# Cross-attention queries by head with the weights stationary, four batches at a time, in place of batch by batch

## The reference

```python
x = _layernorm(x + _L0_attn_ref(x, w_q, w_k, w_v, w_o), axis=-1)
# cross-attention, 16 heads of 128
q = (hidden_states @ Wq + bq).reshape(b, s, NH, HD).transpose(0, 2, 1, 3)
q = _rmsnorm(q, qn_w)      # q * rsqrt(mean(q*q) + 1e-6) * qn_w, for each token and head
scores = jnp.einsum('bhsd,bhed->bhse', q, k) * scale
```

## Time and profile before

| | us |
|---|---|
| median of three runs | 1571.53 |
| the profiled execution | 1568.75 |
| its span, first to last instruction | 1566.9 |
| TensorE busy | 1454.7 (93%) |
| VectorE busy | 951.6 (61%) |
| ScalarE busy | 662.6 (42%) |
| GpSimd busy | 647.5 (41%) |

### The profile page before, as it was taken

One profiled execution on the slowest core, in us unless ns is written; L12 is line 12 of the kernel. 1 busy time (PEld: TensorE's weight loads), 2 busy tenths in 40 slices (PEclk: granted clock), 3 DMA queues, 4 the chain that ended last, 5 costly groups with the idle time before them and its releaser, 6 DMA issues. The chain is left out here.

```text
span 1566.9 us, 25497 instructions
## 1 busy us (share of the span) xinstructions
PE 1454.7 (93%) x8673; PEld 1178.6 (75%) x8673; DVE 951.6 (61%) x3585; ACT 662.6 (42%) x1789; POOL 647.5 (41%) x1000
## 2 busy tenths in 40 slices
PE   7999999999988889999999999999999999399976
PEld 7677767767766678888888888888888887277854
DVE  3766566566566676556655566556655574743357
ACT  4444343343352444344444444444434445243246
POOL 1334234334334454434444444434443435264164
PEclk9999999999999999999999999999999999699999
DMA  6311221221232431121111121211212113485363
GB/s 211 117 64 64 95 74 64 96 74 64 82 129 74 161 109 46 60 62 56 55 44 62 57 64 35 72 56 56 61 44 62 57 42 113 153 239 163 110 215 119
DMA packets 60790, 140.43 MB, mean 90 GB/s; under 512 B 10165, under 2 KB 20761, under 8 KB 59666
## 3 DMA queue, kind: packets, MB, share of 16 engines
q1 hardware_dynamic: 56086, 123.85, 23.8%
q0 software_dynamic: 4576, 14.95, 3.5%
HBM read 94.31 MB, written 44.46 MB: 89 GB/s over the span
## 5 line engine op out<-in xcount | busy, mean ns | idle before, releaser
L1281 POOL TENSOR_TENSOR b_pcarry<-b_half 128x1 f32<-128x1 f32 x173 | 47.1, 273 | 382.0 <-DVE b_rinv L1151 343.8
L1039 ACT ACTIVATE b_probs<-b_probs,b_nmax 100x361 f32<-100x361 f32 x256 | 152.0, 594 | 72.5 <-DVE b_nmax L1145 72.1
L71 PE MATMUL bank<-b_kTh,b_q 128*100 128x362 f32 x512 | 171.2, 335 | 6.4 <-issue 4.8
L1145 DVE CUSTOM_DVE_ANT_0 b_probs<-bank,b_mask 100x361 f32<-100x361 f32 x256 | 135.5, 529 | 49.9 <-issue 41.8
L1306 POOL TENSOR_SCALAR b_probs<-b_probs,b_rinv 100x361 f32<-100x361 f32 x256 | 163.5, 651 | 0.0
L1138 DVE TENSOR_TENSOR b_pTl<-bank,b_pTh 121x400 fp32r<-121x400 f32 x192 | 109.8, 572 | 52.4 <-ACT b_pTh L1034 52.4
L1034 ACT ACTIVATE b_pTh<-bank 121x400 fp32r<-121x400 f32 x192 | 96.7, 504 | 92.6 <-PE bank L871 87.9
L1080 ACT ACTIVATE b_oTh<-bank,b_bv 128x400 fp32r<-128x400 f32 x64 | 38.1, 595 | 222.6 <-PE bank L71 222.6
L871 PE MATMUL bank<-ident,b_probs 100*121 100x100 f32 x768 | 109.7, 265 | 4.3 <-POOL b_probs L1306 3.3
L871 PEld LDWEIGHTS bank<-ident,b_probs 100*121 100x121 f32 x768 | 106.9, 185 | 6.8 <-POOL b_probs L1306 4.5
L71 PE MATMUL bank<-b_Woh,b_oTh 128*100 128x512 f32 x256 | 110.6, 432 | 1.4 <-DVE b_oTl L1209 1.4
(11 more groups left out here) (259 smaller groups left out, 3901.0 us busy)
## 6 DMA issues: line engine op xcount, KB each, us to landing
b_q<-q_d SPq DMA_DIRECT2D x64, 400.0 KB, 3.2
q_d<-a_qo SPq DMA_DIRECT2D x62, 400.0 KB, 2.4
b_ctxr<-in_ctxT SPq DMA_DIRECT2D x48, 242.0 KB, 4.0
y_d<-c_y SPq DMA_DIRECT2D x32, 256.0 KB
c_Eraw<-in_expert_w SPq DMA_DIRECT2D x10, 512.0 KB, 7.4
a_stage<-in_Wq SPq DMA_DIRECT2D x4, 1024.0 KB
stage<-in_Wo SPq DMA_DIRECT2D x8, 512.0 KB, 4.5
a_xTr<-in_xT SPq DMA_DIRECT2D x8, 400.0 KB
```

Of the source, the lines that this page charges most:

```text
L71: mm = eng.matmul(out, lhsT=l(c), rhs=r(c), start=first and k == 0, stop=last and k == n - 1)
L1039: act.activation(p, p, ACT.Exp, scale=-1.0, bias=nmax[:, s % 2, h:h + 1], accum_out=psums[:, s % 2, h:h + 1]).then_inc(e_rdy, 1)
L1145: dve.tensor_tensor_reduce(out=probs[:, s % 2, h, 0:SE], in0=s_bank[h % 2][0:S, 0:SE], in1=mask_s[:], scale=-1.0, scalar=BIG, op0=ALU.add, ...
L1281: pool.tensor_tensor(pcarry[:, k:k + 1], half_s[:, 0:1], half_s[:, 0:1], ALU.add)
```

## The change

The query projection no longer goes with one batch. It waits until four batches (400 tokens, `GT`) have their normed rows, kept transposed and split in `x1Th`, `x1Tl` (two sets). Then it goes by heads: 64 steps m, 16 for each group of four batches. In `query_head(m)` the 128 columns of Wq of one head are the weights and the 400 tokens move; the result stands with the head's 128 values on the partitions, so no transposes are needed. VectorE adds the bias (`queries`), ScalarE and GpSimd each square it (`squares_hi`, `squares`), VectorE takes the difference as the low part (`squares_lo`), and two products with a matrix of ones (`square_sums`) put the sum of squares on every partition. ScalarE takes the root as logarithm and exponential (`root_log`, `root_exp`), VectorE scales (`scaled_queries`), ScalarE writes the high part (`queries_hi`) and GpSimd the low one (`queries_lo`). SP stores two heads at a time in four DMAs of 200 KB, in runs of 800 bytes.

Batches 0 to 3 have no heads, batch 4 has three, each later one four (`heads(i)`), and 17 are left behind the last batch, with the splits of the next phase's context and weights and its three key products among them. The loop of batches is written out. The next pair's projection stands whole behind PV. The bias comes as 128 x 16.

```diff
+GB, HB = 4, 4
+GT = GB * S
+KV_FRAME, CTX_FRAME = (50, 52, 56, 58), (48, 50, 55)
...
+        def heads(i):
+            return [m if m >= 0 else None for m in range(HB * (i - GB) - 1, HB * (i - GB) + HB - 1)]
+        def q_bank(m):
+            return bank[4 + m % 2]
+        def ss_bank(m):
+            return q_bank(m) if m < TAIL else bank[2 + m % 2]
...
+            def store_q(p):
+                sp.wait_ge(q_lo, 2 * p + 2)
+                group, kv, half = p // 8, p // 2 % 4, p % 2
+                for b in range(GB):
+                    dst = q_d[(GB * group + b) * XKV + kv][:, :, half * 2 * S:(half + 1) * 2 * S]
+                    sp.dma_start(dst, qo[:, p % 2, b].bitcast(F32)).then_inc(q_out[p % 2], 16)
...
+            sp.wait_ge(v_done, B)
+            for n in range(2):
+                sp.dma_start(head_raw[:, n], head.pieces[n][0]).then_inc(head.w_raw[n], 16)
+            sp.wait_ge(x1_rdy, B)
+            sp.dma_start(x1_d[B - 1], x1_s[:]).then_inc(x1_out, 16)
+            sp.wait_ge(oT_done, B)
+            sp.wait_ge(qx_done, XH * (B // GB - 1))
+            for n in range(2):
+                sp.dma_start(head.ctxr[:, n], ctxT[n]).then_inc(head.ctx_in[n], 16)
+            for m in range(TAIL, NQ):
+                if m % 2:
+                    store_q(m // 2)
+                for n in range(2):
+                    if m == KV_FRAME[n] + 3:
                         sp.wait_ge(head.w_lo, n + 1)
-                        sp.dma_start(head.pieces[2 + n][1], head.pieces[2 + n][0]).then_inc(head.w_raw[n], 16)
-                if is_int and i == B - 1:
+                        sp.dma_start(head_raw[:, n], head.pieces[2 + n][0]).then_inc(head.w_raw[n], 16)
+                if m == CTX_FRAME[0] + 3:
                     sp.wait_ge(head.ctx_lo, 1)
...
+            def query_head(m):
+                group, kv, cols = m // XH, m // XG % XKV, slice(m % XG * XHD, (m % XG + 1) * XHD)
+                if m % XH == 0:
+                    pe.wait_ge(x1T_lo, GB * (group + 1))
+                if group == 0 and m % XG == 0:
+                    pe.wait_ge(w_lo, 3 + kv)
+                if m >= TAIL + 2:
+                    pe.wait_ge(q_ev, m - 1)
+                elif m >= 2:
+                    pe.wait_ge(ln_set, m - 1)
+                product3(pe, q_bank(m)[:, 0:GT], lambda c: Wqh[:, kv, c, cols], lambda c: Wql[:, kv, c, cols],
+                         lambda c: x1Th[group % 2][:, c, :], lambda c: x1Tl[group % 2][:, c, :], range(DC)).then_inc(qx_done, 1)
+            def square_sums(m):
...
+                pe.wait_ge(sq_hi, m + 1)
+                if m >= TAIL + 2:
+                    pe.wait_ge(ln_set, m - 1)
+                pe.wait_ge(sq_lo, m + 1)
+                pe.matmul(ss_bank(m)[:, 0:GT], lhsT=ones_r[:], rhs=qsh[:], start=True, stop=False)
+                pe.matmul(ss_bank(m)[:, 0:GT], lhsT=ones_r[:], rhs=qsl[:], start=False, stop=True).then_inc(ss_done, 1)
...
+                if m[0] is not None:
+                    if m[0] >= 1:
+                        square_sums(m[0] - 1)
+                    query_head(m[0])
...
+                if m[1] is not None:
+                    query_head(m[1])
+                    if m[0] is not None:
+                        square_sums(m[0])
...
+                if m[2] is not None:
+                    query_head(m[2])
+                pe.wait_ge(v_ev, i + 1)
+                pe.wait_ge(pt_ev, 4 * i + SR)
...
+                if m[1] is not None:
+                    square_sums(m[1])
+                if pair + 1 < NPAIR:
+                    if par == 0:
+                        project(pair + 1, wk_s, range(DC), wk_in)
+                    else:
+                        project(pair + 1, wq_s, range(DC), wq_in)
+                if m[3] is not None:
+                    query_head(m[3])
+                    square_sums(m[2])
...
+            t = TAIL
+            square_sums(t - 1)
+            query_head(t)
+            keep_busy(pe, bank[3][:, 0:P], ident_s, 8)
+            transpose_x1(B - 1)
+            keep_busy(pe, bank[3][:, 0:P], ident_s, 8)
+            for m in range(t + 1, NQ):
+                query_head(m)
+                square_sums(m - 1)
+            context_keys(0)
+            square_sums(NQ - 1)
+            context_keys(1)
+            context_keys(2)
...
+            def squares_hi(m):
...
+                act.wait_ge(q_ev, m + 1)
+                wait(act, ss_done, m)
+                act.activation(qsh[:], qb[:, m % 2], ACT.Square).then_inc(sq_hi, 1)
+            def root_log(m):
...
+                act.wait_ge(ss_done, m + 1)
+                wait(act, q_rdy, m - 1)
+                act.activation(qrs[:, m % 2], ss_bank(m)[:, 0:GT], ACT.Ln, bias=rms_eps_s[:, 0:1]).then_inc(ln_set, 1)
+            def root_exp(m):
...
+                act.wait_ge(ln_set, m + 1)
+                act.activation(qrs[:, m % 2], qrs[:, m % 2], ACT.Exp, scale=-0.5).then_inc(qrs_set, 1)
+            def queries_hi(m):
...
+                act.wait_ge(q_rdy, m + 1)
+                p = m // 2
...
+                if m % 2 == 0:
+                    wait(act, q_out[p % 2], 16 * GB * (p // 2))
+                act.activation(qo[:, p % 2, :, 0, m % 2 * S:(m % 2 + 1) * S], qn[:, m % 2].rearrange("p (b t) -> p b t", b=GB),
+                               ACT.Copy).then_inc(q_hi, 1)
...
+                root_log(before)
+                root_exp(before)
+                exponent(i, 0)
+                exponent(i, 1)
+                if i >= 1:
+                    rows_hi(i - 1)
+                squares_hi(m[0])
+                queries_hi(before - 1)
+                exponent(i, 2)
+                exponent(i, 3)
+                if i == 1:
+                    split_hi(5)
+                act.wait_ge(v_done, i + 1)
+                act.activation(v_s[:], bank[7][0:S, :], ACT.Copy).then_inc(v_ev, 1)
+                root_log(m[0])
+                probs_T(i, 0)
+                probs_T(i, 1)
+                squares_hi(m[1])
+                root_exp(m[0])
+                probs_T(i, 2)
+                probs_T(i, 3)
+                if i == 0:
                     split_hi(2)
+                queries_hi(before)
+                squares_hi(m[2])
+                act.wait_ge(oT_done, i + 1)
+                act.activation(oTh[:].rearrange("p c t -> p (c t)"), bank[7][:, 0:DC * S], ACT.Copy).then_inc(oT_hi, 1)
+                root_log(m[1])
+                root_exp(m[1])
+                queries_hi(m[0])
+                if par == 1 and pair + 1 < NPAIR:
                     scaled_q(pair + 1, 0)
                     scaled_q(pair + 1, 1)
                     split_xT(pair + 1)
+                if i == 0:
                     split_hi(3)
                     split_hi(4)
+                queries_hi(m[1])
+                squares_hi(m[3])
+                root_log(m[2])
+                root_exp(m[2])
+            t = TAIL
+            root_log(t - 1)
+            root_exp(t - 1)
+            queries_hi(t - 2)
+            squares_hi(t)
+            queries_hi(t - 1)
+            rows_hi(B - 1)
+            for m in range(t + 1, NQ):
+                squares_hi(m)
+                root_log(m - 1)
+                root_exp(m - 1)
+                if m >= t + 2:
+                    queries_hi(m - 2)
+                if m in KV_FRAME:
+                    context_weights_hi(KV_FRAME.index(m))
+            root_log(NQ - 1)
+            root_exp(NQ - 1)
+            queries_hi(NQ - 2)
+            queries_hi(NQ - 1)
...
+            def queries(m):
...
+                dve.wait_ge(qx_done, m + 1)
+                wait(dve, q_rdy, m - 1)
+                dve.tensor_scalar(qb[:, m % 2], q_bank(m)[:, 0:GT], bq_s[:, m % XH:m % XH + 1], None, ALU.add).then_inc(q_ev, 1)
+            def squares_lo(m):
...
+                dve.wait_ge(sq_hi, m + 1)
+                dve.wait_ge(sq_set, m + 1)
+                dve.tensor_tensor(qsl[:], qsq[:], qsh[:].bitcast(F32), ALU.subtract).then_inc(sq_lo, 1)
+            def scaled_queries(m):
...
+                wait(dve, q_lo, m - 1)
+                dve.wait_ge(qrs_set, m + 1)
+                dve.scalar_tensor_tensor(out=qn[:, m % 2], in0=qb[:, m % 2], scalar=qkw_s[:, 3:4], in1=qrs[:, m % 2],
+                                         op0=ALU.mult, op1=ALU.mult).then_inc(q_rdy, 1)
...
+                    residual(i - 1)
+                masked(i, 0)
+                if i >= 1:
+                    statistics(i - 1)
+                masked(i, 1)
+                scaled_queries(before)
+                if i >= 1:
+                    apply_norm(i - 1)
+                masked(i, 2)
+                invert_sums(i, 0)
+                masked(i, 3)
+                queries(m[0])
+                invert_sums(i, 1)
+                if i >= 1:
+                    rows_lo(i - 1)
+                if i == 1:
+                    split_lo(4)
+                invert_sums(i, 2)
+                squares_lo(m[0])
+                invert_sums(i, 3)
```

(70 more changed lines are left out.)

540 lines of the change are left out of this document (202 added, 338 removed).

## The result

The changed kernel takes 1593.33 us (median of four runs, 1589.74 to 1599.89) against 1571.91 us for the kernel before on the same chip: a ratio of 1.0135, 95% interval 1.011 to 1.016, so slower. The forecast was 1592. The profiled execution took 1589.74 us (span 1587.9), 21.0 us more span than before.

A forecast was written before the change was run, and what follows sets the result against it. TensorE's own work was taken to bound a batch. 44.3 + 68.5 + 25.5 + 9 x 27.65 + 7 + 47.4 = 441.6 us, with the tail 540.6, 20.4 later than before: forecast 1592 us, range 1553 to 1612.

The forecast's parts named there:

- the tail: Behind the last batch's output product: 17 heads, splits, late loads and final stores take 99 us, against 31.2 before.
- Batches without heads: Batches 1 to 3: the softmax chain is bare, 22.2 us a batch including 2 for the clock; together 68.5.
- Batches with heads: Batches 5 to 13: four heads each, 27.65 us, TensorE's work 24.9 of it, plus 0.7 a batch for the clock.
- 43 us less work: First phase, TensorE: cheaper query products and no query transposes, less the added products with ones, net 43 us.
- The input load behind the stores: Batches with heads, SP queue: an input load sits behind the query stores, charged 1 us in all.
- The loop was put at 3.5 us: Tail: one head's eviction, square, log, exponential, scale and split in turn take 3.44 us, plus 0.06 for the port.
- VectorE's back-to-back pair isn't broken into: SBUF port: whichever engine begins first keeps the other out, so GpSimd can't get between two consecutive VectorE instructions.
- splits and loads with the clock behind them: Tail: context and weight splits and two late weight loads (+5.9 each) add 20.5 us, the clock 6 more.
- The 6 us for the clock: Tail: TensorE stands still for up to 5 us at splits and loads, so its clock falls, +6 us.
- A: Whole kernel, faster: few port collisions, clock holds, loads in time; batches 27.0, tail 76, time 1554 us; chance 0.25.
- B: Whole kernel, slower: every batch trips the clock fully and the head's chain runs late; batches 29.5, time 1609; chance 0.2.
- C: Whole kernel, in between: loads on time and half of the clock losses gone cancel the rest, 1572 us; chance 0.1.

The follow-up runs named there:

- e4: Changed kernel, with the next input load issued between the two halves of the odd batches' stores from batch 5 on; ratio 1.0019 to the kernel before.
- e2: Changed kernel, with GpSimd behind the last batch waiting for head m's low squares before the low part of query head m-2; ratio 1.0089 to the kernel before.
- e7: Changed kernel with e1, e3, e4, context loads first and GpSimd's context split behind its squares and low part; 1555.36 us, ratio 0.9897 to the kernel before.
- e5: Changed kernel with e1 and e3 together; ratio 0.9998 to the kernel before.
- e10: e7 with GpSimd's context split between its squares of head m and low part of head m-2; 1544.57 us, ratio 0.9866 to the kernel before.
- e12: The kernel of e10 run once more, on one chip with e11; 1543.58 us, ratio 0.9872 to the kernel before.
- e3: Changed kernel, with the third and fourth weight pieces loaded as soon as their buffer half is free; ratio 1.0070 to the kernel before.
- e1: Changed kernel, with VectorE behind the last batch taking head m's low squares before head m-1's scaled product; ratio 1.0042 to the kernel before.
- e11: The kernel of e7 run once more, on one chip with e12; 1545.47 us, ratio 0.9888 to the kernel before.
- e6: Changed kernel, with the two first context blocks loaded ahead of the weight pieces, the bias and the store of x1; ratio 1.0105 to the kernel before.

## Why the prediction was right

The sum came out within 1.5 us, but that is partly luck: the last output product was put 7.8 us too late, the tail 4.3 too short and the later phases 3.8 too short, and these cancel.

| term | predicted | measured |
|---|---|---|
| scores of batch 1 start | 44.3 | 45.0 |
| batches 1 to 3 | 68.5 | 68.3 |
| batch 4 | 25.5 | 24.3 |
| batches 5 to 13 | 255.9 | 250.6 |
| batches 14, 15 | 47.4 | 45.7 |
| last product ends | 441.6 | 433.8 |
| tail to phase two | 99 | 103.3 |
| later phases, longer by | 0 | 3.8 |

**Batches without heads.** Right in length and cause: 24.0, 21.5 and 22.8 us, the clock 0.86, 0.92 and 0.85. The 32 products of probabilities with V take 1.56 us there and 0.89 in batches with heads.

**Batches with heads.** The mechanism was right, two sizes were not. An odd batch is 26.35 us, where 27.65 and another 0.7 for the clock were charged: the clock never falls in it (1.00), and TensorE is idle for 0.9 us in all where 1.8 were given to the split of the sums alone. Its work there is 25.4 us (24.9 predicted). For the whole phase 43 us less work were predicted and TensorE's busy time fell by 20.2; the lower clock (0.96 against 0.99) is part of the difference, and how much isn't separated. The input load behind the stores was there, but given 1 us in all: e4 shows 13.3, by 2.2 to 5.0 us in each of the four even batches. Two errors of opposite sign.

**The tail.** Start and end: head 48 evicted 9.5 us behind the product (8.1 predicted), head 63 at 89.3 (87), phase two 14.0 behind that (12). Between, 15 heads took 79.7 us; 79 were predicted, and this is the agreement that owes most to luck. The loop was put at 3.5 us with 0.06 for the port; it is 4.2 to 4.5. The step that failed is "VectorE's back-to-back pair isn't broken into": L743 starts 0.4 us into L620 and L613, the second of the pair, is held until 512.60 + 1.14 = 513.74; with its own 0.57 that is 514.31, and it ended at 514.17. e2 shows the price, 0.83 us a head. The remaining durations were near: log 578 ns (500), exponential 537, copy 521, scaled product 635 (630), eviction 624 (570), GpSimd's two 853 and 1115 (1030 both). Against this, splits and loads with the clock behind them cost some 15 us on top of the longer loop and not 26.5. The two iterations with a load are 8.7 and 8.6 us (predicted near 9), but only 4.2 more than a normal one. The splits at heads 50 and 52 cost about 2.0 and 1.2 where 2.3 each were given. The stop for the first context block, 2.7 us in the iteration of head 49, was no term of the sum; a late split was given 2.1 there. The 6 us for the clock can't be read by themselves: it was 0.63 and 0.70 in the iterations of heads 50 and 52, and stands alone only in that of head 60, 0.4 us longer than the next with 0.58 granted instead of 1.00.

The Trainium skill (SBUF — State Buffer, "Who interferes with whom") says that the engine which loses the port stands still for the other's whole instruction. The trace agrees with the row just worked out. What I added, that two instructions in a row keep the port, is not on that page and is wrong here.

**The later phases** are 3.8 us longer by the profile, from phase two's first load on: 1050.8 against 1046.9. Up to the load of `c_xg`, 974.4 us behind that mark against 972.0, it is 2.4, of which 1.5 come in the set-up (first x1 load 32.3 against 30.8). This is no price of the change that can be named: in the experiments, whose code is the same from there on, the stretch takes 1047.9 (e7) to 1057.6 us (e5), and 1038.0 to 1041.2 in e10 to e12. Its spread is larger than the error of the whole forecast.

**The rivals.** Nothing of A came true but the fast batches. B fell with a clock of 1.00 in the odd batches. C would have needed loads in time: e3 and e4 added, 6.4 and 10.8 us, are 17 us of the 21, though no run has just these two, so the case between was nearer than its chance of 0.1 suggests. What the change loses is not owed to its arithmetic but to four orders in queues, each a few lines, and e7 has it 1.0% faster than before.

## What to carry to other kernels

When work is moved behind the last batch, it loses the cover of the others, and the order within each engine's queue becomes the time. Write down the loop of one item over all engines, take every instruction out of it that another order allows (one swap on VectorE: 4.49 to 3.10 us an item), and put each load where its buffer comes free rather than behind a store that waits for results. Test the waits together: where a load is issued behind a store of results, the chain from those results to its landing has a length of its own, so that heads made faster ahead of it are in part waited back (e1, e2). With the weights early, the two context edits took the tail from 84.7 (e5) to 80.7 us (e7, which has the input early too, worth 0.4 there by itself), against 2.2 for them alone.

## What the runs showed of the hardware

- A GpSimd instruction with SBUF operands that becomes ready during a VectorE instruction gets the port before the next one of VectorE's queue, even where the two stand back to back. L613 took 1.40 to 1.42 us in all 14 heads of the tail in which it stood so behind L620 with L743 ready, and 0.56 to 0.63 in all of e2, where GpSimd is made to wait.
- The price falls on whichever comes second. L743 takes 1.03 to 1.05 us in e2's tail, 1.12 to 1.14 in the changed kernel, where it starts in the end of L620, and 1.47 once in e7, where VectorE's low squares start with it. VectorE's split of a weight piece and GpSimd's of a context block both grow where they meet, from 1.21 and 1.20 us:

```profile
458.80 1.60 DVE L551 TENSOR_TENSOR b_Wkl<-b_head_raw,b_Wkh 128x1024 fp32r<-128x1024 f32 x1
```
```profile
459.41 2.11 POOL L717 TENSOR_TENSOR b_ctxl<-b_ctxr,b_ctxh 128x484 fp32r<-128x484 f32 x1
```

- ScalarE's and VectorE's prices at 128x400: log 578 to 583 ns, exponential and square 537, copy 521 to 529, scaled product of two SBUF tiles 632 to 635 (657 in e2), eviction with a bias 624 to 632 (means of groups).
- A stretch with the same instructions and the same waits can run at either clock, and one kernel shows both: batches 14 and 15 took 22.8 us each at 1.00 in e11 and 24.4 at 0.93 in e7. In the tail a head with 0.50 granted took 5.27 us and with 0.65 4.51 (head 54 in e6 and in the changed kernel). What decides it isn't shown.
- In phase three the first ten profiles have gaps of 6.7 to 10.8 us on ScalarE ahead of copies from PSUM, and e10 to e12 have none, with the same kernel (e7 and e11) and the same chip number. They are large beside what is compared here; only ratios to a kernel that runs beside it, or marks ahead of that phase, tell kernels apart.
